# Where the shared expert's kept halves stand between the pages of a routed expert block: before behind every third page and six at the end, now behind every second page and none at the end

## The reference, cut to what matters

```
xn   = layernorm(x) * w + b
h_t  = tanh(h_{t-1} @ A.T + u_t),  u = xn @ (Ws + Wi).T + bs + bi      (16 states, 256 steps)
x1   = layernorm(x + (H @ Wo.T + bo) * sigmoid(xn @ Wg.T + bg) + x)
s    = softmax(x1 @ gate_w.T);  the two best of s + gate_b, weighted with s
e(x) = silu((x @ w1 + b1) * (x @ w3 + b3)) @ w2 + b2                   (128 -> 176 -> 128)
out  = layernorm(x1 + sum over the two chosen of s_e * e_e(x1) + e_shared(x1))
```

## Time and profile before

| | us |
|---|---|
| median of 3 runs | 509.47 (509.14 to 511.59) |
| the profiled execution's own time | 509.49 |
| its span in the profile | 507.8 |
| outside the span | 1.69 |
| PE busy in the span | 448.0 (88%) |
| DVE, ACT, POOL busy | 345.5, 336.5, 301.2 |

### The profile page before, as it was taken

How to read it: one execution, slowest core, us unless ns; L and a number is a source line. 1 busy time by engine, 2 the same in 40 slices (tenths; PEclk the granted TensorE clock), 3 DMA queues, 4 the chain that set the end, 5 groups by cost and what they waited for, 6 DMA issues and landing times. The chain is left out here.

```text
span 507.8 us, 11172 instructions
## 1 busy us (share of the span) xinstructions
PE 448.0 (88%) x2842; PEld 349.3 (69%) x2842; DVE 345.5 (68%) x1554; ACT 336.5 (66%) x870; POOL 301.2 (59%) x332
## 2 busy tenths in 40 slices
PE   5879999999999988887798998779999999998981
PEld 3546766666666666676697887658888888776640
DVE  5454679898988889856766774244454468777882
ACT  3645777777777776454566676447777777776574
POOL 4100003777776776476677777777767777775241
PEclk9978999999999999889999999899999999999996
DMA  3673112333333222397456476557777778891642
GB/s 112 130 230 110 57 42 79 85 116 91 99 99 92 79 80 76 107 265 217 127 151 194 132 219 178 163 163 214 228 212 228 213 255 301 251 335 54 220 176 104
DMA packets 58228, 79.81 MB, mean 157 GB/s; under 512 B 11182, under 2 KB 37803, under 8 KB 58166
## 3 DMA queue, kind: packets, MB, share of 16 engines
q1 hardware_dynamic: 49516, 62.17, 42.4%
q0 software_dynamic: 8640, 16.93, 9.6%
q10 hardware_dynamic: 10, 0.00, 0.0%
HBM read 47.85 MB, written 25.84 MB: 145 GB/s over the span
## 5 line engine op out<-in xcount | busy, mean ns | idle before, releaser
L616 POOL DMA_INDIRECT ys<-yp,xp x142 | 143.0, 1007 | 51.2 <-issue 37.9
L609 POOL DMA_INDIRECT xs<-x,place_i x128 | 124.7, 974 | 58.9 <-issue 22.7
L690 ACT ACTIVATE hT<-pu,bu 16x32 f32<-16x32 f32 x256 | 78.7, 308 | 60.9 <-PE pu L1388 56.1
L681 ACT ACTIVATE hid<-z 128x512 f32<-128x512 f32 x103 | 64.7, 628 | 68.8 <-DVE z L1114 68.2
L1388 PEld LDWEIGHTS pu<-hT,aT 128*66 128x66 f32 x512 | 54.5, 141 | 58.0 <-ACT hT L690 52.8
L1388 PE MATMUL pu<-hT,aT 128*66 128x32 f32 x512 | 78.6, 241 | 12.0 <-ACT hT L690 11.7
L597 POOL TENSOR_TENSOR rstd_in<-ve_in,neghalf 128x4 f32<-128x4 f32 x16 | 16.4, 1027 | 66.0 <-DVE ve_in L824 65.9
L1109 DVE SCALAR_TENSOR_TENSOR z<-p,wp,t3a 128x256 f32<-128x256 f32 x50 | 24.1, 482 | 39.3 <-ACT t3a L669 35.9
L1326 PE MATMUL ph<-xpT,wp 128*128 128x256 f32 x142 | 43.9, 391 | 5.9 <-DVE z L1114 5.8
L1333 PE MATMUL py<-wp,hid 128*128 128x128 f32 x200 | 41.9, 292 | 7.9 <-DVE yp L1135 4.9
L1333 PEld LDWEIGHTS py<-wp,hid 128*128 128x128 f32 x200 | 31.6, 193 | 18.6 <-DVE yp L1135 8.3
(11 more groups left out here) (303 smaller groups left out, 1069.7 us busy)
## 6 DMA issues: line engine op xcount, KB each, us to landing
wp<-packed SPq DMA_DIRECT2D x71, 320.0 KB, 3.6
xp<-xs SPq DMA_DIRECT2D x71, 130.0 KB, 2.9
weights<-ys SPq DMA_DIRECT2D x10, 512.0 KB, 4.5
xt<-in_L_attn_x SPq DMA_DIRECT2D x16, 256.0 KB, 3.1
x<-x SPq DMA_DIRECT2D x16, 256.0 KB, 2.7
x<-ys SPq DMA_DIRECT2D x6, 512.0 KB, 7.5
packed<-weights SPq DMA_DIRECT2D x1, 2560.0 KB, 8.6
ys<-yp,xp POOLq DMA_INDIRECT x142
```

The source lines that it names most:

```text
L609: g.indirect_dma_start(out=xs[:, :], out_offset=bass.IndirectOffsetOnAxis(ap=place_i[b % NB][:, c, t * Q + q:t * Q + q + 1], axis=0), in_= ...
L616: g.indirect_dma_start(out=ys[:, :], out_offset=bass.IndirectOffsetOnAxis(ap=xp[j % NX][:, h, DEST:DEST + 1].bitcast(int32), axis=0), in_= ...
L681: nc.scalar.activation(hid[u % NH][:, :], z[u % 2][:, :], ACT.Silu).then_inc(hid_ready, 1)
L690: nc.scalar.activation(hT[k % 2][0:N, c], pu[k % 2][0:N, c], ACT.Tanh, bias=bu[:, 0:1]).then_inc(h_ready, 1)
```

## The change: two numbers of the unit table

`AFTER` goes from 6 to 0 and `BETWEEN` from 3 to 2. All 19 kept halves are put among the pages, behind every second one, for the pages 0 to 37; the pages 38 to 70 follow each other, and nothing of the shared expert stands behind page 70. No operation, size or buffer changes. The start slots of all pages from page 2 on move back: page 33 from 294 to 299, page 70 from 333 to 339; page 70's send moves from slot 337 to 344, and with it the slots of all sums by 7. The stages also come out one slot deeper for all pages: down product and result stand 4 slots behind a page's start, and before 3.

```diff
-    APART, FILL, AFTER, BETWEEN = 0, 0, 6, 3
+    APART, FILL, AFTER, BETWEEN = 0, 0, 0, 2
```

## The result

The changed kernel takes 515.92 us (median of 4 runs, 515.29 to 517.02), against 509.42 us before: ratio 1.011, interval 1.0075 to 1.015. Forecast were 506.6 us and a range up to 512.3. The profiled execution took 516.12 us, its span is 514.4 us; forecast 504.9.

The account below looks back on a forecast made before the run. PE and the ACT-DVE loop set the pace, with POOL's full queue costing 10.8 us between 310 and 345. Marks 312.6, 462.8, 467.4, 480.6, 503.7, plus 1.2 clock, gave span 504.9; with 1.69 outside, 506.6 us; 8-in-10 range 502.0 to 512.3.

Parts of the forecast that it names:

- Step 1: Up to slot 282's z: two more shared halves instead of pages, -0.5 and -1.0 us, mark 312.6 instead of 314.14.
- R: Mark of the last page's result, behind which only sums and stores remain; forecast 467.4 us, before 461.80.
- Step 2: POOL's queue of scatters and pages, 310 to 345 us: POOL stays full, last scatter ends 325.9, stall 3.0 instead of 10.8.
- Step 3: From slot 282 to the last page's z: 49 pages, 9 halves, stall and sums take 150.2 us, mark 462.8.
- Step 4: Last page's z to its result: one slot deeper, bounds 4.25 and 6.8, taken as 4.6 us.
- Step 5: From the last page's result to the fold of sum 10: 13.2 us instead of 22.9, late loads hidden behind ACT.
- Step 6: From the fold of sum 10 to the end: the same 23.1 us as before, ending at 503.7.
- Step 7: PE's gap of 4.9 us before the fold of sum 10 lowers the granted clock: 1.2 us, new end 504.9.
- Rival C: Tail eats the middle's gain: late loads contend, 1.3 us late, clock low twice as long; 510.1 us, chance 0.17.
- Rival D: Other work, not POOL, holds the units of 310 to 345 us, so no gain there; 514.4 us, chance 0.03.

Follow-up runs that it names:

- clear kernels: Changed kernel, first halves behind pages 2, 5, 7, 9, ..., so slots 254 and 258 keep their z; with AFTER 6 509.22 us, with AFTER 3 503.99 us.
- clear kernel with AFTER 0: Changed kernel with only the halves' phase moved (behind pages 2, 5, 7, 9, ...), so slots 254 and 258 keep their z: 510.30 us.

## Why the prediction was wrong, step by step

- *Step 1, z of slot 282: the step that failed*, 318.02 instead of 312.6. It said that only the two more shared halves change anything up to there, and that the deeper stages change no pace. The slots before 260 were taken as full, and no term stood for the clock ahead of the tail. In the clear kernels whose clock stayed up (AFTER 6 and 3) the mark is 313.6: 1.0 of the miss is the arithmetic, 4.4 are the hole and the falls of the clock beside it. The hole of slot 258 is 2.2 of them; the falls can do as much alone, since the clear kernel with AFTER 0 passed the mark at 318.42 after two falls and without a hole. Its profiled run still ended 5.8 us earlier than that of the kernel after: from the mark to R it took 151.3 us against 155.7, by 2.96 instead of 4.31 from the last z to R (three-slot stages) and by 17.3 instead of 20.1 for the seven units behind slot 282 (its longest wait for `ys` there was 1.4 us instead of 3.4), and 1.7 in the tail. So the holes are dear by what they bring with them, and the deeper stages do cost, at the last page. In time, holes against none: 5.6 us and 4.9 us. How each divides into hole, clock and depth in the runs without a profile is not known.
- *Step 2, POOL's queue.* The waits are right in number and size (one or two, some 4 us; measured two, 4.4 us, the longer at page 23 as forecast), but "POOL stays full" was not: its pauses between 235 and 262 us grew from 5.3 to 13.7 us, and the last scatter into `xs` started at 329.67 instead of 325. Without the holes it started at 325.5.
- *Step 3*: 151.4 us instead of 150.2. Pages keep their 2.53 us.
- *Step 4*: 4.31 against 4.6. *Step 5*: 13.0 against 13.2, but with less to spare than it said: the first late load went out at R + 8.4, where the step had it landed, since the last send began at R + 6.3 instead of R + 1.7, and the median landing grew from 4.5 to 5.6 us. It came level with ACT. The R + 1.7 stood against the step's own rows, by which the last send came 3.6 us behind the last result (461.80 to 465.39).
- *Step 6, "the same 23.1 us": the second that failed.* The six loads came together behind the last send, which was 6.3 us behind R and not 1.7; stores queued behind them. Worth 2.6 to 2.8 us in after.
- *Step 7, the clock*: 1.7 us against 1.2, in the place where it was looked for and once more behind R, though the gap of PE was 2.83 us and not 4.9, because the first folds were late and slow (474.0 to 477.2, clock 0.50). The folds behind it took 1.30 and 1.49 us instead of 0.81. The Trainium skill (TensorE: Matmul & The Clock Gate, "Why this matters for your kernels") warns of long idle gaps between matmul bursts; the traces agree in part, since the clock also fell behind a wait of 1.59 us (474.51) and stayed up behind one of 3.05 us (before with AFTER 3).
- Rival C had the tail's two mechanisms, with the lateness put into the fold's wait instead of the stores, and 510.1 us. Rival D's 514.4 is the nearest number, by a reason that the waits refute. No rival had the held bank or a fall of the clock ahead of slot 282.

## What to carry to other kernels

A unit that needs one resource less (here no transposing bank) may be what fills the slots in which that resource is taken; before moving such units, list the slots that the plan leaves empty, not only the order of instructions. Where one engine needs a little more per item than the loop (2.58 against 2.53 us), the fillers are the places in which it catches up without making the loop wait, so they belong ahead of the first reader of its results. Fillers behind the last item are cheap up to the size of the gap there (three of six), and taking them all away bunched, here, the loads that they had kept apart.

## What the runs showed of the hardware

- The granted clock can fall in one kernel and stay in another at the same point of the same work (0.60 and 1.00 from 230 to 238 us), and a fall there cost 3.0 us at slot 257's z, a second 1.7 more at slot 260's.
- It fell behind waits of PE of 1.6 and 2.8 us in after (474 and 488 us), and stayed up behind 2.5 us in the clear kernel and 3.05 us in the kernel before with AFTER 3.
- Stores issued between loads of 512 KB left their buffers some 2 us late per store (ACT's waits) while the DMA share was 0.83 over 13 us; with one store between two loads, 2.5 us of such waits in one of four runs and none in three.
- Four of the six sets of runs fell on chips on which the same kernel takes 628 instead of 510 us, with waits of up to 9.4 us that have no name in the trace; one edit measured four times gave ratios from 0.986 to 1.0005 there.
